# Node products of a graph network: weight copies on ScalarE, the residual added in thirteen pieces, one read of the spill flag

## What is computed

```python
for l in range(3):
    f1 = relu(x[row] @ nb_W[l] + nb_b[l])
    f2 = relu(x[col] @ self_W[l] + self_b[l])
    h = relu(concatenate([f1, f2], axis=1) @ att1_W[l] + att1_b[l])
    log_alpha = (h @ att2_W[l] + att2_b[l])[:, 0]
    mask = clip(sigmoid(log_alpha) * (ZETA - GAMMA) + GAMMA, 0.0, 1.0)
    rowsum = segment_sum(mask, row) + 1e-06
    d = clip(rowsum ** (-0.5), 0.0, 10.0)
    vals = mask * d[row] * d[col]
    x = segment_sum(vals[:, None] * x[col], row)
    out = out + x
```

## Time and profile before

| | us |
|---|---|
| median of 3 runs | 4171.06 (4166.67 to 4172.17) |
| profiled execution | 4178.5 |
| its span | 4176.8 |
| TensorE busy | 3757.2 (90%) |
| VectorE busy | 3586.6 (86%) |
| GpSimd busy | 2799.7 (67%) |
| ScalarE busy | 2013.5 (48%) |

### The profile page before, as it was taken

How to read it: one execution, slowest core, us unless ns; L and a number is a source line. 1 busy time by engine, 2 the same in 40 slices (tenths; PEclk the granted TensorE clock), 3 DMA queues, 4 the chain that set the end, 5 groups by cost and what they waited for, 6 DMA issues and landing times. The chain is left out here.

```text
span 4176.8 us, 261652 instructions
## 1 busy us (share of the span) xinstructions
PE 3757.2 (90%) x99727; PEld 3572.9 (86%) x99728; DVE 3586.6 (86%) x5801; ACT 2013.5 (48%) x5437; POOL 2799.7 (67%) x4756
## 2 busy tenths in 40 slices
PE   5888668888779999899988999999997999989998
PEld 4777568888759999899978999999996999989997
DVE  7999968888768888799987888799996788879998
ACT  4898858888721111466641111156663111136664
POOL 2777533333235666899974666699995566679998
PEclk7888889999979999999999999999998999999999
DMA  1000089999727777566645777666662677756665
GB/s 36 14 15 15 13 263 334 341 341 331 280 93 249 244 241 251 172 182 180 180 114 184 240 246 245 232 161 180 180 180 86 232 250 240 248 183 182 180 180 145
DMA packets 586273, 800.11 MB, mean 192 GB/s; under 512 B 126790, under 2 KB 528154, under 8 KB 586170
## 3 DMA queue, kind: packets, MB, share of 16 engines
q1 hardware_dynamic: 550106, 719.89, 55.3%
q0 software_dynamic: 36064, 78.85, 6.3%
HBM read 672.34 MB, written 126.04 MB: 191 GB/s over the span
## 5 line engine op out<-in xcount | busy, mean ns | idle before, releaser
L1329 PE MATMUL pre_ps<-rows_a,hot_ab 128*128 128x64 bf16 x21609 | 1302.8, 194 | 47.3 <-ACT rows_a L1425 26.3
L1329 PE MATMUL pre_ps<-table,hot_ab 128*128 128x64 bf16 x21609 | 1302.1, 194 | 6.7 <-issue 6.7
L1553 POOL TENSOR_TENSOR message<-message 128x448 f32<-128x448 f32 x1029 | 1302.6, 1303 | 5.4 <-ACT message L1478 4.3
L1329 PEld LDWEIGHTS pre_ps<-rows_a,hot_ab 128*128 128x128 fp8e4 x21609 | 1131.3, 98 | 76.0 <-issue 52.6
L1329 PEld LDWEIGHTS pre_ps<-table,hot_ab 128*128 128x128 fp8e4 x21609 | 1133.7, 98 | 7.2 <-issue 7.2
L1614 DVE TENSOR_TENSOR message<-message 128x448 f32<-128x448 f32 x1029 | 1003.5, 976 | 17.3 <-POOL message L1553 17.3
L1478 ACT ACTIVATE message<-pre_ps,mask 128x64 f32<-128x64 f32 x3087 | 745.3, 312 | 441.3 <-PE pre_ps L1376 416.5
L1602 DVE SCALAR_TENSOR_TENSOR message<-pre_ps,w 128x448 f32<-128x448 f32 x1029 | 642.5, 624 | 288.3 <-PE pre_ps L1329 210.0
L1376 PE MATMUL pre_ps<-table,hot_ab 128*128 128x64 bf16 x21609 | 804.0, 194 | 60.8 <-DVE message L1631 45.9
L1376 PEld LDWEIGHTS pre_ps<-table,hot_ab 128*128 128x128 fp8e4 x21609 | 755.1, 98 | 84.1 <-issue 76.7
L1585 DVE TENSOR_REDUCE logit<-message 128x7 f32<-128x448 f32 x1029 | 626.2, 609 | 0.0
(11 more groups left out here) (177 smaller groups left out, 5088.2 us busy)
## 6 DMA issues: line engine op xcount, KB each, us to landing
hot_ab<-hot_scratch SPq DMA_DIRECT2D x2058, 224.0 KB, 3.9
hot_scratch<-hot SPq DMA_DIRECT2D x343, 336.0 KB, 5.9
both<-hot_scratch SPq DMA_DIRECT2D x147, 784.0 KB, 5.1
places<-slots_scratch POOLq DMA_DIRECT2D x196, 224.0 KB, 6.4
places<-slots_scratch POOLq DMA_DIRECT2D x98, 336.0 KB, 7.3
slots_scratch<-bins SPq DMA_DIRECT2D x392, 16.0 KB, 1.4
out<-res SPq DMA_DIRECT2D x1, 1536.0 KB
raw<-in_src SPq DMA_DIRECT2D x1, 768.0 KB
```

The lines of the kernel that those rows point to most:

```text
L1329: last = nc.tensor.matmul(pre_ps[g][:, j, :], hot[:, b, g, end, j * P:(j + 1) * P].bitcast(FP8), table, start=end + part == 0, stop=end == ...
L1553: pool.tensor_tensor(message[:, g, :, 1, :], message[:, g, :, 0, :], top[:, g, :, 0, :, 1], ALU.subtract).then_inc(s["rest_ready"], 1)
```

## The change

The six weight copies go from VectorE to ScalarE, ahead of its first copy of turn_ps, with w3 last. A new one-column Sigmoid stands at the end of ScalarE's program in `node_products`; it reads `pcol` and writes `spare`, which nothing reads. GpSimd adds `cur` to `res` in 13 pieces, one for each span: the piece of span m-1 stands ahead of the wait for the first part of span m, right behind `rest` of span m-1, and the last piece behind the last `rest`. The spill flag is read into registers once, between `first_table` and `build_and_sum`, and all seven places branch on that.

```diff
@@ spilled_edges
-    spilled = nc.values_load(k.some_spill[0:1, 0:1], skip_runtime_bounds_check_because="only tested")
-    with nc.If(spilled > 0):
+    with nc.If(k.spilled > 0):
@@ allocate_layers
+    k.spare = sb("spare", [P, 1], F32)
@@ node_products, scalar
+                at = bass.ds(l, 1)
+                nc.scalar.activation(k.b1[:, :], k.all_b1[:, at], ACT.Copy)
+                nc.scalar.activation(k.b3[:, :], k.all_b3[:, at], ACT.Copy)
+                for own, every in ((k.w1, k.all_w1), (k.w2, k.all_w2), (k.b2, k.all_b2), (k.w3, k.all_w3)):
+                    last = nc.scalar.activation(own[:, :].unsqueeze(1), every[:, at, :], ACT.Copy)
+                last.then_inc(s["weights"], 1)
                 for m in range(n + 1):
...
                     if m >= 1:
                         relu(m - 1)
+                nc.scalar.activation(k.spare[:, :], k.pcol[:, :], ACT.Sigmoid)
@@ node_products, gpsimd
-                pool.tensor_tensor(k.res[:, :], k.res[:, :], k.cur[:, :], ALU.add).then_inc(s["res_added"], 1)
+                def add_rows(m):
+                    a, z = spans[m]
+                    at = slice(a * D, z * D)
+                    pool.tensor_tensor(k.res[:, at], k.res[:, at], k.cur[:, at], ALU.add).then_inc(s["res_added"], 1)
+
                 for m, (a, z) in enumerate(spans):
+                    if m >= 1:
+                        add_rows(m - 1)
                     pool.wait_ge(s["first_ready"], m + 1)
...
-                pool.wait_ge(s["res_added"], 1)
+                add_rows(n - 1)
+                pool.wait_ge(s["res_added"], n)
@@ node_products, vector
                 dve.memset(k.spill_sums[:, :], 0.0)
-                at = bass.ds(l, 1)
-                dve.tensor_copy(k.b1[:, :], k.all_b1[:, at])
-                dve.tensor_copy(k.b3[:, :], k.all_b3[:, at])
-                dve.tensor_copy(k.w1[:, :].unsqueeze(1), k.all_w1[:, at, :])
-                dve.tensor_copy(k.w3[:, :].unsqueeze(1), k.all_w3[:, at, :])
-                dve.tensor_copy(k.b2[:, :].unsqueeze(1), k.all_b2[:, at, :])
-                dve.tensor_copy(k.w2[:, :].unsqueeze(1), k.all_w2[:, at, :]).then_inc(s["weights"], 1)
                 dve.wait_ge(s["weights"], 1)
@@ gnn
         first_table(nc, k)
+        k.spilled = nc.values_load(k.some_spill[0:1, 0:1], skip_runtime_bounds_check_because="only tested")
         build_and_sum(nc, k)
```

## The result

The changed kernel takes 4177.48 us (median of 20 runs, 4169.94 to 4181.52) beside 4166.65 us for the kernel before (20 runs): a ratio of 1.0022, 95% interval [1.0016, 1.0028], or +9.2 us [6.7, 11.7]; the two medians lie 10.8 us apart. The forecast was +7.6 us and 4178.7. It is slower, by just over the 0.2% that can be told from no change.

The account below looks back on a forecast made before the run. TensorE was taken to set the node products' pace at 2.58 us a span, GpSimd and VectorE close behind. Node products +9.5, flag -1.9, table 0 gave +7.6 us: 4178.7 us on the 4171.06 median, range 4163 to 4185.

Parts of the forecast that it names:

- The mechanism: Body of the node products: pieces and VectorE's casts take turns, so a 3.02 us loop replaces TensorE's 2.58 as bound.
- Two of the marks named for it: Node products: first L1129 near 3.6 us after the table load begins; cast of part 1 starting only at the add's end.
- first product sooner: Start of the node products, weights copied by ScalarE: 4.3 us gained in layer 1, 0.75 each in layers 2 and 3.
- pieces, in the stage: Node products: the thirteen adds lengthen the loop of GpSimd and VectorE, costing 5.1 us a layer.
- flag: Spill flag read once instead of seven times: six reads of 0.32 us leave the path, -1.9 us.
- gate's table: Start of the masks: L1425's table load goes, priced at 0 because row 1 waits for hot_ab; -1.28 a layer kept for range.
- the last span, priced at 0.79: End of the node products: 0.60 us lost for the piece ahead of the last `rest`, 0.19 for its own piece.
- The rival in which the loads pass through: Masks: row 1's wait moves with TensorE's earlier start; total +3.8 us, 4174.9 us, chance 0.12.
- The clock's rival: Masks, row 1: a longer standstill lets TensorE's clock fall in every layer; total +12.7 us, 4183.8 us, chance 0.16.
- The hidden pieces: Node products: casts go on beside an add, the loop stays at 2.42 us; total -7.7 us, 4163.4 us, chance 0.12.

Follow-up runs that it names:

- the third experiment: The kernel before with the single flag read and the tail Sigmoid; VectorE keeps the weights, GpSimd's one add waits for them: 0.9972, 4159.50 us.

## Why the prediction was right, and where its steps were not

**The mechanism** held: a cast is held up beside an add, and the closed chain of GpSimd and VectorE replaced TensorE's 2.58 us. Two of the marks named for it came out otherwise: the cast of part 1 starts beside the piece and is stretched, where it was to start at the piece's end, and the first L1129 comes 2.87 us after the table load begins, for "near 3.6" (the prediction's own sum gives 3.3). "SBUF — State Buffer" of the Trainium skill, Who interferes with whom, was set against the change for just this; the cast at 0.94 us beside the piece agrees with it. The sizes, by the rows of the stage and loop, in us over three layers:

| term | forecast | measured |
|---|---|---|
| first product sooner | -5.8 | 4.54 + 0.81 + 0.85 = -6.2 |
| pieces, in the stage | +15.3 | 3.92 + 3.93 + 3.91 in the body, 0.1 a layer at the end: +12.1 |
| flag | -1.9 | -1.9 by its rows; -2.9, 3.5 to either side, by its own runs |
| gate's table | 0 | 3 x -0.9 = -2.7, about 2.3 to either side |
| rows of the masks | none | 0.03 to 0.04 x 48 rows x 3 = +4 to +6 |
| sum | +7.6 | +5 to +7; the runs say +9.2 [6.7, 11.7] |

**Pieces.** The loop was forecast at 3.02 and is 2.92 us: I added the piece's whole 0.60, but the cast of part 1 ends 0.29 us behind the piece, not its own 0.42 behind it, and 0.52 is what the chain lost. That, on ten intervals, makes most of 5.1 against 4.0 a layer; the rest is the last span, priced at 0.79.

**The head.** The number was right and the reason half right. The gain is not ScalarE's: the weights left on VectorE start the product 1.05 us sooner still in layer 1 (1.96 for 3.01) once the add is out of the way. The runs cannot tell whether that gain reaches the time: with one add it is 0.9972 for 0.9978 [0.9969, 0.9987], with pieces 1.0013 [1.0005, 1.0022] for 1.0022, and the 3.6 and 4.3 us of the rows would fit both.

**The table** is the step that failed: "price the load at 0", since TensorE stands still in row 1 anyway. Had the earlier start been lost in that standstill, the standstill would end no sooner after SyncE's first load. It ends 0.94, 1.62 and 1.25 us sooner in the three layers of the changed kernel, and the fifth load comes 0.9 us sooner in the mean of all profiles. The rival in which the loads pass through was nearer the truth: about -2.7, with 2.3 to either side, where it had -3.8. The table load at L1425 did go, as forecast. By the rule of the Trainium skill that loads are placed block by block ("ScalarE activation tables: per-element evaluation and per-set limits", Table sets in the compiler and the runtime) it would have stayed; this program does not agree with the rule.

**The clock's rival** did not come: in layer 2 the standstill grew to 2.46 us, and the clock kept 1.00 after it. **The hidden pieces** are excluded by the cast's row.

**That the total came out** is owed in part to luck, in errors of opposite sign: the forecast was too high by 3.2 us for the pieces and by 2.7 for the table, and too low by the 4 to 6 us in the rows of the masks that no step foresaw. The absolute time came closer still (4177.48 for 4178.7) because the later median of the kernel before was 4.4 us lower than the one the forecast was put on. And the rows do not account for all. Three timed pairs with and without pieces give 17 to 21 us, the rows of stage and masks 16 to 20. But the pieces alone, in the kernel before, should come to 9.6 us gained at the head and 12 lost, +2.4, and measured +7.5 [3.8, 11.3], with no slower rows in its profile. Pieces and flag (+3.1 by the same reckoning, +7.9 [4.2, 11.7] measured) and the changed kernel with the weights on VectorE (+0.9, and +5.4 [2.1, 9.2]) miss some 5 us as well. All three have the pieces, and all three have VectorE's copies and with them the earliest first product; the third experiment, which has the copies without the pieces, misses 3 us (-14.8 by the rows, -11.7 [-15.8, -7.1] measured), which its interval covers. What these 5 us are stays open.

**A version that beats both** is the changed kernel with one add at the head: 0.9978 and 0.9968 in two sets of runs, 9 and 13 us under the kernel before. The one with the add behind VectorE's weight copies (0.9972) is as good.

## What to carry to other kernels

An idle microsecond of GpSimd is no room for an add if VectorE's copies or casts close the same chain: add the turns of both engines around the loop first (here 2.42 us of 2.58) and see what is left over. In this kernel the long add was cheaper in one piece, at a moment when VectorE has nothing to do, than in thirteen beside its casts. And where single profiles differ by more than the change is worth, compare stretches between like marks, and one part of the change at a time.

## What the runs showed of the hardware that was not expected

- A cast of 512 columns beside a GpSimd add of 256 takes 0.94 to 0.96 us for 0.41 to 0.43, in either of two casts, and a GpSimd add of 256 columns reads 0.72, 0.92 or 1.17 us by what VectorE does meanwhile.
- One Sigmoid in the tail of a stage took away two table loads of the next, L1425's and L1421's: six loads fewer for three more.
- TensorE begins each stage of node products at its lower clock (granted 0.50 in the first 3 us from the first product in all 42 stages of these profiles), and when the clock rises differs by stage and by execution. In layer 1 of the kernel before the granted clock was 0.50 from 1166 to 1174, with TensorE busy for 7.93 of the 8 us, 0.60 in the mean of the next 6 us, and 1.00 from 1180 on; with the flag alone it was 0.50 for the first 7.6 us and 0.91 in the mean of the next 5. From the first product to the third `rest` it took 13.86 to 17.34 us in the 42 stages (before 16.4 to 16.7 in all three layers, the flag alone 14.2 to 14.4). That is up to 3 us a layer, more than most terms here. With one profile of each kernel it is not shown that no edit moves it.
- A row of the masks, untouched by any edit, took 9.79 to 9.85 us in the fourteen kernels; over 147 rows 0.06 us are 9 us. The slower ones are those with both pieces and one flag read, and why is open.
